# Cross attention and an emulated MXFP8 feed-forward on one Trainium2 core: probabilities scaled in place and turned by float32 transposes with the identity, row-statistics squares kept in the down results' buffer, and every engine's order rewritten

## The chip, the core and the metric

The kernel runs on 1 core of one Trainium2 chip, as five programs side by side: TensorE (PE), VectorE (DVE), ScalarE (ACT), GpSimd (POOL) and SyncE (SP, which here only issues DMAs). The metric is the device time of one execution in microseconds; smaller is better. Before the change it is 609.74 us, the median of 3 runs (608.04 to 609.96).

## What is computed

```
x = x + xattn(layernorm(x), ctx, Wq, bq, Wk, bk)      # x: 4 x 512 x 512, ctx: 4 x 512 x 256
x = x + ffn(layernorm(x), gate_w, up_w, down_w)       # inner size 2048

xattn: query = ctx @ Wq.T + bq;  key = ctx @ Wk.T + bk;  energy = query @ key.T
       attention = softmax(energy, axis=-1);  result = logits @ attention.T
ffn:   gate = mx(x) @ mx(gate_w).T;  up = mx(x) @ mx(up_w).T
       out = mx(silu(gate) * up) @ mx(down_w).T
mx(t): blocks of 32 along the last axis, scale = max|block| / 448, round(t / scale) to float8_e4m3, times scale
```

## The kernel before

Everything is float32 outside and float16 pairs (a high and a low part) inside the feed-forward. There are four batches b of four row tiles of 128 rows, so 16 row tiles r = 4b + lt. The work has these pieces:

- **Attention of batch b** (float32 on PE). `project(b, i)` makes queries and keys of 128 x 512, `energies(b, nt)` a tile of energies, DVE's `row_max` the maximum, ACT's `exponential(b, nt)` the unnormalized probabilities in `probs[b]` with their sum, DVE's `row_sum(b)` the reciprocals. ACT's `weigh(b, nt)` builds a diagonal matrix of 128 x 128 from the identity `idf` and these reciprocals, and PE's `turn_probs(b, nt)` multiplies four blocks of 128 x 128 of the probabilities with it, which turns and normalizes them at once. ACT's `take_probs` copies the result into `AT`, and PE's `attend(b, lt)` (4 matmuls of 128 x 512, at L711) multiplies the input's columns with it. DVE's `add_attended` adds that to the rows, scaled by the reciprocal standard deviation of the row.
- **That deviation** comes from ACT: `row_means(b, half)` and `row_variances(b, half)` pass over the rows with an accumulator; the passes' outputs themselves are never read. The second half ends with a logarithm and an exponential (L975, L976), which give `xrstd_ready`.
- **Quantizing**. Twelve weight units u = 0 to 11 (gate and up of column block c are units 2c and 2c+1, down is 8 to 11), four row batches, and 16 hidden rows go the same way: DVE reduces, scales (L1590, L1537 or L1647), ACT takes magnitudes (L926), DVE rounds (L1458, L1459) and multiplies back (L1605, L1550, L1659). Then the high part is cast by ACT (`unit_hi` L944, `rows_hi` L1074, `hidden_hi` L1114), POOL issues an accumulating DMA that leaves the rest (`unit_rest` L585, `rows_rest` L589, `hidden_rest` L593), the low part is cast (`unit_lo` L950, `rows_lo` L1080), and SP turns both by DMA transposes (L401, L406 for units; L420, L425 for rows; L439, L444 for hidden rows).
- **Feed-forward on PE**. `product(r, c)` is 24 float16 matmuls of 128 x 512 (gate, then up; for each the high rows with high weights, high rows with low weights, low rows with high weights). It waits for `nT_in` (rows turned) and `wT_in` (units turned). `down(r)` is 48 matmuls from the turned hidden row, and `down_last` the same in two halves.

PE's eight banks are given out by a written table `bank_uses`: each string is the list of uses of one bank in order (p, e, t, a for the attention's steps, g and u for gate and up, d for down), and `take_bank` waits until the use ahead of it has been read. The order on each engine is likewise written out call by call; nothing is decided at run time, and an instruction that waits holds all behind it on its engine. SP's and POOL's lists hold the DMAs in the order in which they are issued, with waits between them.

Of the kernel before, what the change touches and what calls it, by code (L numbers as in the profile page):

```python
# [10 lines left out]
ACT = mybir.ActivationFunctionType  # L11
# [21 lines left out]
def xattn_ffn(nc, xrows, xcols, ctxT, consts, units, out):  # L33
# [22 lines left out]
    products = [(3, 0), (1, 0), (0, 0), (2, 0), (3, 1), (2, 1), (6, 0), (6, 1), (4, 0), (4, 1), (5, 0), (2, 2),  # L56
# [5 lines left out]
    nth = {rc: n for n, rc in enumerate(products)}  # L62

    rounds = ("u0 u1 u2 n0 u3 n1 u4 u5 u6 u7 u8 u9 u10 u11 h0 h1 n2 h2 h3 h4 n3 h5 h6 h7 h8 h9 h10 h11 h12 h13 h14"
              " h15").split()
# [3 lines left out]
        ("p0.0 p2.0 e2.0 a0.3 a1.0 a2.2 g1.0 a3.2 g2.1 g4.1 u6.2 g0.2 u0.3 u3.3 u7.1 g8.0 u9.1 g11.0 u12.0 u14.2"  # L69
         " u13.1 g8.2 u10.2 u15.0 d9").split(),  # L70
        ("p0.1 e1.0 e2.1 t1.0 a1.1 t3.0 g0.0 u2.0 g4.0 u2.2 g0.1 u6.3 u1.3 g7.1 d0 g9.1 u10.0 d4 g10.3 u15.1 d11").split(),
        ("e0.0 e1.1 t0.3 a0.2 e3.0 t2.2 a2.0 g3.0 u1.0 g6.0 u4.1 u3.2 u0.2 u1.1 g4.3 u7.2 u8.0 g9.3 g11.1 g12.1"
         " g14.2 u13.0 g12.3 u10.1 d6 g15.3 d14").split(),
        ("e0.1 e1.2 a0.0 t1.3 a1.3 t3.3 a3.3 u2.1 g5.0 g5.1 g5.3 g1.2 u4.2 g7.3 g8.1 g9.2 u11.0 u12.1 g14.3 g13.1"
         " u12.3 g10.2 g15.0 u15.2 d13").split(),
        ("e0.2 e1.3 a0.1 t2.0 t2.3 a2.1 u3.0 g2.0 g6.1 u5.0 g5.2 u5.3 g1.3 u4.3 u7.3 g9.0 u9.3 u11.2 u14.1 g13.0"
         " u13.3 g10.1 u11.3 g15.2 d12").split(),
        ("e0.3 t0.0 t0.2 e2.2 t1.1 t2.1 e3.3 t3.1 u0.0 u6.0 g2.2 u5.1 g6.3 u1.2 g7.0 g2.3 u8.1 g10.0 g11.2 u14.0"
         " u12.2 g13.3 u8.3 g11.3 d8 d15").split(),
        ("p1.0 p2.1 t0.1 p3.1 t1.2 a1.2 t3.2 a3.0 g3.1 u6.1 g6.2 u5.2 g0.3 g3.3 u7.0 u2.3 u9.0 d2 d3 g12.0 g14.1"  # L80
         " g12.2 u13.2 g8.3 d5 g15.1 u15.3").split(),
        ("p1.1 p3.0 e2.3 e3.1 e3.2 a2.3 a3.1 u3.1 u4.0 g3.2 u0.1 g1.1 g4.2 g7.2 d1 u9.2 u11.1 g14.0 u14.3 g13.2"
         " u8.2 u10.3 d7 d10").split(),
# [9 lines left out]
    with ExitStack() as stack:  # L93
# [62 lines left out]
        diagonal = [[h[:, nt, 512 + n * P:512 + (n + 1) * P] for nt in range(LT)] for n in range(B)]  # L156
# [68 lines left out]
        diagonal_ready = sem("diagonal_ready")  # L225
# [105 lines left out]
        def _(sp):  # L331
# [113 lines left out]

            load_slice(0)
            load_ctx(0)
            load_consts()
            load_half(0)
            load_rest(0)  # L450
            load_rows(0)
            load_ctx(1)
            load_unit(1)
            load_ctx(3)
            load_ctx(2)
            load_rows(1)
# [461 lines left out]
        def _(act):  # L918
# [1050 lines left out]
```

## Time and profile before

| | value |
|---|---|
| median of 3 runs | 609.74 us (608.04 to 609.96) |
| profiled execution: span | 608.0 us (the fastest of the three runs took 608.04 us) |
| PE busy | 600.6 us, 99% |
| DVE busy | 484.0 us, 80% |
| ACT busy | 309.2 us, 51% |
| POOL busy | 44.8 us, 7% |
| granted TensorE clock | 0.999 |

The profile gives each engine's busy time, the same in 40 slices of about 15.2 us, the waits with what ended them, and every instruction with its start. A page's matmul durations include the pipeline's depth; the distance from one matmul's start to the next, read from the timeline, is what one costs when they follow each other. Waits that DVE or ACT have cost nothing by themselves while PE goes on.

### The profile page before, as it was taken

How to read it: one execution, taken by the hardware profiler on the slowest of the kernel's cores; microseconds unless marked ns; L12 is line 12 of the kernel's file. 1: busy time of each engine (PE TensorE's matmuls, PEld its weight loads, DVE VectorE, ACT ScalarE, POOL GpSimd, SP SyncE). 2: the span in 40 equal slices, each digit the busy share in tenths (PEclk: the TensorE clock that was granted, in tenths of full speed). 3: DMA queues.
4: the chain of work that ended last, by engine and by line, in shares of the span. 5: the costliest groups of instructions: out<-in, count | busy, mean ns of one | idle time of the engine just before them, and what ended most of it. 6: DMA issues, size and time to landing. Idle time of an engine off the chain costs nothing.

```text
span 608.0 us, 7215 instructions
## 1 busy us (share of the span) xinstructions
PE 600.6 (99%) x2683; PEld 282.3 (46%) x2683; DVE 484.0 (80%) x455; ACT 309.2 (51%) x463; POOL 44.8 (7%) x60
## 2 busy tenths in 40 slices
PE   8999999999999999999999999999999999999998
PEld 3456554444444444444444444444444444444446
DVE  4999998899999999988999985131148899989740
ACT  3999989553555555853475532431121515254520
POOL 0000002100000001010110201000000000001100
PEclk9999999999999999999999999999999999999999
DMA  8989869989988978867445655750010334557691
GB/s 314 396 206 275 234 177 256 280 193 249 208 207 209 219 159 210 174 140 171 124 112 97 148 112 113 165 86 0 1 19 0 53 69 83 90 105 101 110 171 35
DMA packets 148162, 92.28 MB, mean 152 GB/s; under 512 B 134304, under 2 KB 134688, under 8 KB 143264
## 3 DMA queue, kind: packets, MB, share of 16 engines
q1 hardware_dynamic: 142656, 63.78, 45.2%
q0 software_dynamic: 5472, 28.05, 19.9%
q8 instruction: 21, 0.34, 0.2%
q14 instruction: 13, 0.11, 0.1%
HBM read 25.76 MB, written 8.39 MB: 56 GB/s over the span
## 4 chain that ended last, share of the span: by engine, by line
PE 85%; DMA 5%; issue 3%; ACT 3%; DVE 1%; SPq 1%; POOL 0%; DVEq 0%; ACTq 0%
PE bank L727 49%; PE bank L739 17%; PE bank L742 9%; PE bank L711 5%; DMA h<-in_ctxT 2%; PE bank L702 1%; PE bank L695 1%; DMA xT<-hT 1%; PE bank L687 1%; PE bank L757 1%; DMA W<-hT 1%; DMA h<-hT 1%; ACT hT L944 1%; PE bank L762 1%; ACT h L987 0%
## 5 line engine op out<-in xcount | busy, mean ns | idle before, releaser
L727 PE MATMUL bank<-gu_hi,xT 128*128 128x512 f16 x1024 | 243.6, 380 | 1.7 <-DMA xT<-hT 1.7
L727 PEld LDWEIGHTS bank<-gu_hi,xT 128*128 128x128 f16 x1024 | 99.9, 98 | 123.4 <-DMA xT<-hT 3.2
L727 PE MATMUL bank<-gu_lo,xT 128*128 128x512 f16 x512 | 131.5, 379 | 0.0
L739 PE MATMUL bank<-dn,hT 128*128 128x512 f16 x480 | 106.1, 379 | 0.0
L1633 DVE SCALAR_TENSOR_TENSOR h<-bank,unscale,silu 128x512 f32<-128x512 f32 x64 | 47.4, 747 | 56.1 <-PE bank L727 36.1
L1088 ACT ACTIVATE silu<-bank,unscale 128x512 f32<-128x512 f32 x64 | 42.8, 679 | 83.4 <-PE bank L727 40.3
L727 PEld LDWEIGHTS bank<-gu_lo,xT 128*128 128x128 f16 x512 | 50.1, 98 | 60.4
L739 PEld LDWEIGHTS bank<-dn,hT 128*128 128x128 f16 x480 | 47.0, 98 | 56.6
L1114 ACT ACTIVATE W<-h 128x2048 f16<-128x2048 f32 x16 | 30.5, 1909 | 68.3 <-DVE W L1665 25.4
L711 PE MATMUL bank<-dn,h 128*128 128x512 f32 x128 | 55.9, 593 | 0.0
L742 PE MATMUL bank<-dn,hT 128*128 128x512 f16 x240 | 54.3, 379 | 0.0
L1458 DVE SCALAR_TENSOR_TENSOR h<-mag,h 128x2048 f32<-128x2048 bf16 x18 | 41.2, 2288 | 9.4 <-ACT mag L926 9.4
L926 ACT ACTIVATE mag<-h 128x2048 bf16<-128x2048 f32 x18 | 34.2, 1903 | 19.5 <-DVE h L1647 14.1
L1459 DVE SCALAR_TENSOR_TENSOR h<-mag,h 128x2048 f32<-128x2048 bf16 x18 | 41.2, 2292 | 0.6
L926 ACT ACTIVATE mag<-W 128x2048 bf16<-128x2048 f32 x14 | 26.7, 1908 | 23.0 <-DVE W L1590 11.9
L711 PEld LDWEIGHTS bank<-dn,h 128*128 128x128 f32 x128 | 24.3, 190 | 29.8 <-issue 29.4
L1665 DVE SCALAR_TENSOR_TENSOR W<-h,W 128x2048 f16<-128x2048 f32 x9 | 20.6, 2289 | 20.9 <-DMA hT<-W 17.4
L1647 DVE TENSOR_TENSOR h<-h,rscale 128x2048 f32<-128x2048 f32 x16 | 36.7, 2292 | 0.5
L1642 DVE TENSOR_REDUCE hscale<-h 128x64 f32<-128x2048 f32 x16 | 36.5, 2281 | 0.3
L1659 DVE TENSOR_TENSOR h<-h,hscale 128x2048 f32<-128x2048 f32 x16 | 36.6, 2288 | 0.2
L742 PEld LDWEIGHTS bank<-dn,hT 128*128 128x128 f16 x240 | 23.5, 98 | 28.3
L1458 DVE SCALAR_TENSOR_TENSOR W<-mag,W 128x2048 f32<-128x2048 bf16 x14 | 32.0, 2286 | 1.0 <-ACT mag L926 1.0
(119 smaller groups left out, 560.1 us busy)
## 6 DMA issues: line engine op xcount, KB each, us to landing
W<-hT POOLq DMA_DIRECT2D x12, 1024.0 KB, 5.9
W<-in_units SPq DMA_DIRECT2D x11, 1024.0 KB, 5.7
h<-W POOLq DMA_DIRECT2D x7, 1024.0 KB, 6.1
h<-in_xcols SPq DMA_DIRECT2D x4, 1024.0 KB, 12.6
out_y<-y POOLq DMA_DIRECT2D x12, 256.0 KB, 6.2
h<-in_xrows SPq DMA_DIRECT2D x2, 1024.0 KB, 11.8
out_y<-h SPq DMA_DIRECT2D x2, 1024.0 KB, 5.5
h<-hT POOLq DMA_DIRECT2D x2, 1024.0 KB, 5.9
```

Of the source, the lines that this page charges most:

```text
L711: last = pe.matmul(bank[:, :], xTf[b % 2][:, j, lt * P:(lt + 1) * P], AT[:, j, :], start=(j == 0), stop=(j == HT - 1))
L727: last = pe.matmul(bank[:, :], xT[:, b % 2, part, k, :], w[:, c, g, j * 512:(j + 1) * 512], start=(j == 0 and not low), stop=(j == HT - 1 ...
L739: pe.matmul(bank[:, :], hT[:, r % 2, 0, k, :], dn[:, w, k, :], start=(k == 0 and w == 0), stop=False)
L742: last = pe.matmul(bank[:, :], hT[:, r % 2, 1, k, :], dn[:, 0, k, :], start=False, stop=(k == IT - 1))
L926: nc.scalar.activation(mag[:, :], v, ACT.Abs, scale=MAGIC).then_inc(mag_ready, 1)
L1088: nc.scalar.activation(silu[:, n % 2, :], bank_of(f"g{r}.{c}")[:, :], ACT.Silu, scale=unscale[:, 2 * c:2 * c + 1]).then_inc(silu_ready, 1)
L1458: then(dve.scalar_tensor_tensor(v, mag[:, :], floor, v, ALU.max, ALU.add))
L1459: dve.scalar_tensor_tensor(v, mag[:, :], floor, v, ALU.max, ALU.subtract).then_inc(mag_used, 1)
L1633: dve.scalar_tensor_tensor(hrow(r)[:, c * 512:(c + 1) * 512], bank_of(f"u{r}.{c}")[:, :], unscale[:, 2 * c + 1:2 * c + 2], silu[:, n % 2, ...
L1642: then(dve.tensor_reduce(s, blocks(row), AX.X, ALU.max, apply_absolute_value=True))
L1647: dve.tensor_tensor(blocks(row), blocks(row), each_block(rscale[:, :]), ALU.mult).then_inc(hv_ready, 1)
L1659: dve.tensor_tensor(blocks(row), blocks(row), each_block(hscale[:, r % 2, :]), ALU.mult).then_inc(hd_ready, 1)
```

## The change

`turn_probs` transposes blocks of probabilities with the identity instead of multiplying with a diagonal matrix. For that `weigh` now scales the probabilities themselves in place (128 x 512 instead of 128 x 128). `row_means` and `row_variances` leave their unread outputs in `y`, the buffer of the down results with two places, instead of in four places in `h`; with the diagonals also gone from `h`, `hidden_of` (DVE, writes a piece of a hidden row into `h`) needs two waits less. The order of the calls on all five engines, the table of banks and some of the waits between DMAs are new.

```
-        diagonal = [[h[:, nt, 512 + n * P:512 + (n + 1) * P] for nt in range(LT)] for n in range(B)]
...
-                pe.wait_ge(diagonal_ready, LT * b + nt + 1)
+                pe.wait_ge(normal_ready, LT * b + nt + 1)
                 for j in range(HT):
-                    last = pe.matmul(bank[:, j * P:(j + 1) * P], probs[b][:, nt, j * P:(j + 1) * P],
-                                     diagonal[b][nt], start=(j == 0), stop=(j == HT - 1))
+                    last = pe.transpose(bank[:, j * P:(j + 1) * P], probs[b][:, nt, j * P:(j + 1) * P], idf)
...
-                    if lt in copied:
-                        act.wait_ge(act_step, copied[lt])
-                    last = nc.scalar.activation(h[:, lt, 0:512], X[b][:, lt * H:(lt + 1) * H], ACT.Copy,
+                    if lt % 2 in copied:
+                        act.wait_ge(act_step, copied[lt % 2])
+                    last = nc.scalar.activation(y[:, lt % 2, :], X[b][:, lt * H:(lt + 1) * H], ACT.Copy,
...
-                nc.scalar.activation(diagonal[b][nt], idf, ACT.Copy, scale=rsum[:, LT * b + nt:LT * b + nt + 1]
-                                     ).then_inc(diagonal_ready, 1)
+                act.wait_ge(exp_ready, LT * b + nt + 1)
+                nc.scalar.activation(probs[b][:, nt, :], probs[b][:, nt, :], ACT.Copy,
+                                     scale=rsum[:, LT * b + nt:LT * b + nt + 1]).then_inc(normal_ready, 1)
...
-                if r < LT and c == 0:
-                    dve.wait_ge(xrstd_ready, B)
-                elif r < LT and c == 1:
-                    dve.wait_ge(probs_turned, LT * B)
-                elif r < LT and c >= 2:
+                if r < LT and c >= 2:
...
             turn_rows_hi(0)
             turn_rows_lo(0)
-            store_rows(1)
+            turn_unit_hi(2)
+            load_columns(3)
...
             load_unit(6)
+            sp.wait_ge(*rows_rest_in(1))
+            turn_rows_hi(1)
+            turn_rows_lo(1)
             store_rows(3)
             sp.wait_ge(*unit_rest_in(4))
-            turn_rows_hi(1)
-            turn_rows_lo(1)
             turn_unit_hi(4)
             turn_unit_lo(4)
             load_unit(7)
...
             rows_rest(1)
+            unit_max(5)
+            pool.wait_ge(nT_in[1], 32)
             unit_rest(4)
-            unit_max(5)
-            unit_max(6)
```

The order of products changes throughout; its first rows, before and after:

```
-    products = [(3, 0), (1, 0), (0, 0), (2, 0), (3, 1), (2, 1), (6, 0), (6, 1), (4, 0), (4, 1), (5, 0), (2, 2),
+    products = [(3, 0), (1, 0), (0, 0), (2, 0), (3, 1), (0, 1), (6, 0), (2, 1), (5, 0), (6, 1), (4, 0), (5, 1),
+                (1, 2), (1, 1), (0, 2), (4, 2), (5, 2), (2, 3), (0, 3), (6, 2), (1, 3), (2, 2), (5, 3), (6, 3),
```

**PE around the first product.** Before the change PE's list around the first product reads as follows; L702 is `turn_probs` of batch 3 (4 blocks each, 16 in all), L711 `attend` (batch 2 ahead of the products, batch 3 behind), L727 the products (3, 0), (1, 0) and (0, 0).

```order
L711 MATMUL bank<-dn,h 128x512 x16
L702 MATMUL bank<-h,gu_lo 128x128 x16
L727 MATMUL bank<-gu_hi,xT 128x512 x4
L727 MATMUL bank<-gu_lo,xT 128x512 x4
L727 MATMUL bank<-gu_hi,xT 128x512 x8
...
L727 MATMUL bank<-gu_hi,xT 128x512 x4
L711 MATMUL bank<-dn,h 128x512 x16
```

With the change the same place reads (L703 is `turn_probs`):

```order
L711 MATMUL bank<-dn,h 128x512 x16
L703 MATMUL bank<-gu_lo 128x128 x8
L727 MATMUL bank<-gu_hi,xT 128x512 x4
L727 MATMUL bank<-gu_lo,xT 128x512 x4
L727 MATMUL bank<-gu_hi,xT 128x512 x8
...
L703 MATMUL bank<-gu_lo 128x128 x4
...
L703 MATMUL bank<-gu_lo 128x128 x4
...
L711 MATMUL bank<-dn,h 128x512 x16
```

Two of the four turnings of batch 3 have moved behind the first product: one stands behind product (1, 0), the other behind (0, 0), and product (2, 0) now stands ahead of `attend` of batch 3.

**ACT behind the high rows of batch 1.** Before, the three calls behind `rows_hi(1)` (L1074) read as follows (L1088 is the silu of a product, L944 `unit_hi(4)`, L1080 `rows_lo(1)`); `row_variances(3, 1)` with its L975 and L976 stood ahead of the first silu.

```order
L1074 ACTIVATE hT<-h 128x2048
L1088 ACTIVATE silu<-bank,unscale 128x512
L944 ACTIVATE hT<-W 128x2048
L1080 ACTIVATE hT<-h 128x2048
```

With the change (L1075 is `rows_hi(1)`, L987 to L976 are `row_variances(3, 1)`, L1081 is `rows_lo(1)`):

```order
L1075 ACTIVATE hT<-h 128x2048
L1089 ACTIVATE silu<-bank,unscale 128x512
L987 ACTIVATE y,gu_lo<-gu_hi,gu_lo 128x512 x2
L975 ACT_TABLE_LOAD
L975 ACTIVATE gu_lo<-gu_lo,eps 128x4
L976 ACT_TABLE_LOAD
L976 ACTIVATE gu_lo<-gu_lo 128x4
L1081 ACTIVATE hT<-h 128x2048
L944 ACTIVATE hT<-W 128x2048
L1089 ACT_TABLE_LOAD
L1089 ACTIVATE silu<-bank,unscale 128x512
```

The last half of batch 3's row statistics has moved behind the first silus, and with it come three table loads more.

**POOL behind the rest of the rows of batch 1.** Before (L589 is `rows_rest(1)`, the first L585 `unit_rest(4)`, the second `unit_rest(5)`, L575 `unit_max`; in brackets the semaphores that are waited for):

```order
L589 DMA h<-hT 128x2048 [waits nhi_ready,wT_in1]
L585 DMA W<-hT 128x2048 [waits whi_ready]
L575 ISA
L575 ISA umax<-smax 128x1 [waits smax_ready] x2
L585 DMA W<-hT 128x2048 [waits whi_ready,wT_in1]
```

With the change:

```order
L589 DMA h<-hT 128x2048 [waits nhi_ready,wT_in1]
L575 ISA
L575 ISA umax<-smax 128x1 [waits smax_ready]
L585 DMA W<-hT 128x2048 [waits whi_ready,nT_in1]
L585 DMA W<-hT 128x2048 [waits whi_ready,wT_in1]
```

`unit_rest(4)` now waits for the low rows of batch 1 to have been turned (`nT_in1`).

## Rows read from the trace of the kernel before

**Rows 1.** The page: busy time of engines, and granted clock in 40 slices.
```profile
PE 600.6 (99%) x2683; PEld 282.3 (46%) x2683; DVE 484.0 (80%) x455; ACT 309.2 (51%) x463; POOL 44.8 (7%) x60
PEclk9999999999999999999999999999999999999999
```

**Rows 2.** Busy time by stretch (us, engine and count, clock, DMA share, GB/s).
```profile
8.00:93.00 85.00, 82.51 (x287) 44.13 (x286) 81.52 (x103) 77.65 (x176) 5.35 (x9) 1.00 0.90 270
140.00:290.00 150.00, 150.00 (x697) 67.95 (x695) 143.17 (x132) 82.57 (x88) 11.98 (x16) 1.00 0.84 196
290.00:608.00 318.00, 315.07 (x1508) 147.16 (x1505) 216.16 (x178) 117.13 (x163) 19.50 (x22) 1.00 0.45 84
```

**Rows 3.** Timeline of PE: start, duration, instruction, idle before.
```profile
5.87 4.02 PE L687 MATMUL bank<-gu_hi,gu_lo 128*128 128x512 f32 x8
49.83 3.74 PE L702 MATMUL bank<-h,dn 128*128 128x128 f32 x32
53.40 1.06 PE L702 MATMUL bank<-h,gu_lo 128*128 128x128 f32 x8
74.20 13.90 PE L711 MATMUL bank<-dn,h 128*128 128x512 f32 x32
87.94 3.73 PE L702 MATMUL bank<-h,gu_lo 128*128 128x128 f32 x32
92.60 1.04 PE L727 MATMUL bank<-gu_hi,xT 128*128 128x512 f16 x4 [0.93 <-DMA xT<-hT]
138.57 1.04 PE L727 MATMUL bank<-gu_hi,xT 128*128 128x512 f16 x4 [0.32 <-DMA xT<-hT]
603.16 1.91 PE L762 MATMUL bank<-dn,hT 128*128 128x256 f16 x16
```

**Rows 4.** Groups by line and shape: weight loads on PE.
```profile
L727 PEld LDWEIGHTS bank<-gu_hi,xT 128*128 128x128 f16 x1024 | 99.9, 98 | 123.4 <-DMA xT<-hT 3.2 <-issue 0.6
L702 PEld LDWEIGHTS bank<-h,gu_lo 128*128 128x128 f32 x64 | 7.8, 192 | 1.4 <-issue 1.0 <-DVE dn L1504 0.2 <-ACT gu_lo L997 0.2
```

**Rows 5.** Timeline of DVE.
```profile
8.22 1.22 DVE L1569 TENSOR_REDUCE scale<-W 128x32 f32<-128x1024 f32 x1 [7.09 <-DMA W<-in_units]
70.89 2.29 DVE L1550 TENSOR_TENSOR h<-h,xscale 128x2048 f32<-128x2048 f32 x1
112.78 2.29 DVE L1550 TENSOR_TENSOR h<-h,xscale 128x2048 f32<-128x2048 f32 x1
149.97 2.28 DVE L1564 TENSOR_REDUCE scale<-W 128x64 f32<-128x2048 f32 x1
```

**Rows 6.** Timeline of ACT.
```profile
75.44 1.89 ACT L1074 ACTIVATE hT<-h 128x2048 f16<-128x2048 f32 x1
83.56 1.26 ACT L1003 ACTIVATE h<-gu_lo 128x128 f32<-128x128 f32 x4
88.22 1.91 ACT L1080 ACTIVATE hT<-h 128x2048 f16<-128x2048 f32 x1 [1.60 <-DMA h<-hT]
92.34 2.54 ACT L1059 ACTIVATE h<-h,nmean 128x512 f32<-128x512 f32 x4
96.70 1.28 ACT L1088 ACT_TABLE_LOAD   x1
115.11 1.91 ACT L1074 ACTIVATE hT<-h 128x2048 f16<-128x2048 f32 x1 [1.67 <-DVE h L1550]
```

**Rows 7.** Timeline of POOL and of SP's queue: DMA issues.
```profile
82.44 0.88 POOL L589 DMA_DIRECT2D h<-hT  x1 [10.01 <-issue]
124.79 0.86 POOL L585 DMA_DIRECT2D W<-hT  x1 [6.17 <-ACT hT L944]
88.21 1.68 SPq L420 DMA_TRANSPOSE xT<-hT  x1
130.63 4.91 SPq L420 DMA_TRANSPOSE xT<-hT  x1
143.40 0.69 SPq L335 DMA_DIRECT2D W<-in_units  x1
184.97 2.24 SPq L406 DMA_TRANSPOSE gu_lo<-hT  x1
```

More of the change, by code:

```diff
@@ L807, in _ @@
             attend(0, 3)
+            energies(3, 0)
+            energies(3, 1)
+            energies(3, 2)
             turn_probs(1, 0)
@@ L854, in _ @@
+            product(1, 2)
+            product(1, 1)
+            product(0, 2)
+            product(4, 2)
+            product(5, 2)
+            product(2, 3)
+            product(0, 3)
+            product(6, 2)
+            product(1, 3)
+            product(2, 2)
             product(5, 3)
             product(6, 3)
-            product(0, 3)
-            product(1, 1)
-            product(1, 2)
-            product(1, 3)
+            product(3, 2)
+            product(4, 1)
             product(3, 3)
-            product(4, 2)
@@ L877, in _ @@
-            down(2)
-            product(11, 0)
-            product(11, 1)
-            product(11, 2)
-            down(3)
-            down(4)
+            product(10, 1)
+            down(2)
+            product(8, 2)
+            product(10, 0)
+            down(3)
+            product(10, 2)
+            product(11, 3)
+            product(11, 1)
+            product(11, 0)
+            product(9, 3)
+            down(4)
+            down(5)
+            product(13, 0)
+            product(12, 1)
@@ L883, in _ @@
+            product(9, 2)
+            product(11, 2)
+            down(6)
+            product(12, 2)
+            product(10, 3)
+            product(13, 2)
+            product(13, 1)
+            product(13, 3)
             product(12, 0)
-            product(12, 1)
             product(14, 0)
+            product(12, 3)
+            down(7)
             product(14, 1)
+            product(14, 3)
             product(14, 2)
-            product(14, 3)
-            product(12, 2)
-            product(13, 0)
@@ L911, in _ @@
+            down(8)
+            down(9)
+            down(10)
+            product(15, 2)
+            product(15, 3)
+            product(15, 0)
             down(11)
@@ L1365, in _ @@
-            hidden_rescale(6)
+            rows_magnitude(3)
+            silu_of(9, 1)
+            hidden_lo(3)
+            silu_of(10, 1)
+            hidden_unscale(4)
+            silu_of(8, 2)
+            hidden_hi(4)
+            hidden_magnitude(5)
+            silu_of(10, 0)
+            rows_hi(3)
+            silu_of(10, 2)
+            silu_of(11, 3)
+            hidden_rescale(6)
+            hidden_hi(5)
+            hidden_magnitude(6)
+            hidden_lo(4)
+            silu_of(11, 1)
@@ L1369, in _ @@
+            silu_of(11, 2)
+            hidden_magnitude(9)
+            hidden_rescale(9)
+            silu_of(12, 2)
+            silu_of(10, 3)
+            take_down(4)
+            silu_of(13, 2)
+            hidden_hi(7)
+            silu_of(13, 1)
+            take_down(5)
+            hidden_magnitude(10)
+            silu_of(13, 3)
             silu_of(12, 0)
-            hidden_lo(5)
-            silu_of(12, 1)
+            hidden_hi(8)
+            hidden_magnitude(11)
+            hidden_hi(9)
@@ new lines, in _ @@
+            hidden_rescale(11)
+            hidden_hi(10)
+            hidden_unscale(8)
+            take_down(8)
+            silu_of(14, 2)
+            silu_of(15, 1)
+            hidden_unscale(9)
+            hidden_rescale(12)
+            hidden_hi(11)
+            hidden_magnitude(13)
+            take_down(9)
+            hidden_rescale(13)
+            hidden_hi(12)
+            hidden_unscale(10)
+            silu_of(15, 2)
+            hidden_unscale(11)
+            hidden_rescale(14)
@@ L1436, in _ @@
+            hidden_unscale(12)
+            hidden_hi(13)
+            take_down(10)
+            silu_of(15, 3)
+            silu_of(15, 0)
+            take_down(11)
+            hidden_unscale(13)
+            hidden_rescale(15)
+            hidden_magnitude(14)
+            hidden_magnitude(15)
+            hidden_hi(14)
+            take_down(12)
+            take_down(13)
+            hidden_unscale(14)
+            hidden_hi(15)
+            add_constant()
+            take_down(14)
             hidden_unscale(15)
-            hidden_hi(15)
```

794 lines of the change are left out of this document (354 added, 440 removed), and 9 rows, old and new, of the table products.

## The prediction, made blind

> **What bounds the kernel now.** I read the page first. PE is busy for 600.6 of 608.0 us and the granted clock is full in every slice, which is the 2.4 GHz level [rows 1]. Then the stretches: from 140 to 290 us PE runs 697 matmuls in 150.00 us, and the rest of the kernel looks the same [rows 2], so from there on PE is the bound and nothing that another engine does is seen. The last matmuls start at 603.16 us [rows 3]; the 3 us behind them are the last sums and the store. The stretch ahead of 93 us is different: DVE is busy for 81.5 and ACT for 77.7 of 85 us beside PE's 82.5 [rows 2]. Three engines are full there at once, and the reader should ask of each of them what it could do if the others were faster.
>
> The first product starts at 92.60 us, after 0.93 us of waiting for turned rows [rows 3]. From there to the end PE waits 0.32 us and hardly more. So the span is (start of the first product) + 515.4 us, of which nearly all is matmuls that the change keeps. This one moment, call it T1, is where the change must be read.
>
> T1's chain: DVE multiplies the rows of batch 0 back, ends at 73.1 [rows 5]; ACT casts them, 75.44 to 77.3 [rows 6]; POOL issues the accumulating DMA at 82.44, it lands at about 88.2, where SP turns the rows [rows 7]; 4.4 us later the product starts.
>
> **The change, part by part.**
>
> *The transposes.* Before, 32 records (16 blocks of 128 x 128) start 3.57 us apart (49.83 to 53.40 [rows 3]): 0.223 us a block, 14.3 us for 64. The trace has no transpose in the transposing mode, so I bound it. Above: the same 0.223 us. Below: a float16 matmul is one pass, 150 us / 697 = 0.215 us for 512 columns, so 128 columns in one pass are 0.054 us. A weight load takes 98 ns in float16 and 192 ns in float32 [rows 4], and one must go with each block. I take 0.1 us, nearer to the low end, since a block then needs one load and one pass. PE's work falls by 64 x 0.12 = 7.9 us, with ends of 0 and 10.8 us.
>
> A rule speaks to this. The Trainium skill, page "TensorE: Matmul & The Clock Gate", section "Terms", calls the transpose mode 4 times faster for FP32. By it a block would be 0.056 us and PE's work 10.7 us less; no row here shows it. If that were all, the span would be 597.3 us.
>
> *But PE's saving lies ahead of T1 and PE doesn't set T1.* Ahead of the first product PE had 83 us of work in 86.7 us. Now it has 73 us (two turnings of batch 3 stand behind it), and T1 waits for DVE and ACT.
>
> *DVE up to the rows of batch 0.* The calls ahead of and with the multiplying back of batch 0 are the same 45 before and now, in another order. They take 64.9 us from 8.22 us on [rows 5], of which some 2 us are waits (1.0 for a magnitude, 0.8 for an attended bank, and small ones). Without any wait they end at 71.1, as before at 73.1. Walking through both lists with the durations of the trace I get one wait of about 1 us for the magnitude of the rows, and 72.5.
>
> *ACT up to casting these rows.* Two calls are moved behind (two halves of variances, 1.4 and 1.9 us, -3.3 us). All 12 `weigh` of batches 0 to 2 stand ahead of it; each grows from 1.26 / 4 = 0.31 us to 2.54 / 4 = 0.63 us, the price of four 128 x 512 passes [rows 6]: +3.8 us. Net +0.5 us on an engine that was busy 62 of 67 us. The walk gives a start of the cast at 73.4 against 75.44, with ends of 71 (no waits at all) and 76. The squares that go to `y` cost nothing: same instructions, and ACT executes them one after the other anyway. So the cast ends at 75.2, 2.1 us earlier.
>
> *The DMA.* Before, 5.1 us passed between the end of the cast and POOL's issue, though POOL shows nothing else [rows 6, 7], then 5.8 us of flight. For batch 1 the issue follows the cast at once. Before, SP had issued a slow load of columns (12.6 us is the median of that kind) just ahead; now that load stands behind the turning of the rows. I take 7 us from the cast to landing instead of 10.9: 82.2 (as before: 86.1). Now PE's list has two turnings of batch 3 ahead of product (3, 0), and their `weigh` stand on ACT behind the low rows, which wait for this landing: 1.8 + 1.5 (means) + 0.4 + 2 x 0.6 us, then the turnings, 0.4. T1 = 82.2 + 5.3, with the hand-overs between engines (some 0.1 us each) and the SP's transpose in parallel (4.4 us) about 88.5. With 86.1 it would be 92. `attend` of batch 2 (13.7 us [rows 3]) ends at 85.6 and doesn't hold it. **T1: -4.1 us**, with ends -6 and 0.
>
> *What is late next.* Two things are due: rows of batch 1, needed by product (6, 0), and the weight units. Up to product (6, 0) PE has attend of batch 3 (13.7) and six products (5.18 each): T1 + 45.3 = 133.8. SP turned these rows at 130.63, behind a store and the rest of unit 4 [rows 7]; now right after their own rest. DVE's list ahead of them has two pieces of hidden rows and one unit's reduction more (+2.9 us), against 4.1 us of waits that it had between 73 and 115. I keep DVE's end at 115.0 as before [rows 5]; cast 1.9, DMA 7, and the turning lands at 129, its low part at 134, which is needed at 135.5. No wait.
>
> Three table loads of 1.28 us [rows 6] come in by the late `row_variances(3, 1)`: they lie on ACT between 117 and 126, where ACT was half idle. They hold `xrstd` of batch 3 until 122; DVE's first addition of batch 3 waits some 1 us, and PE's banks don't need it sooner.
>
> Units 6 and 7 are the tight place. Product (2, 3) is now 18th behind T1, where before a product with c = 3 came 19th: it is due at T1 + 0.4 + 13.7 + 17 x 5.18 = T1 + 102.2 = 190.7; before at 200. Unit 7's low part was turned from 184.97 on [rows 7] and lands 4.3 us later, at 189.3. POOL's new wait puts the rest of unit 4 behind the turned low rows of batch 1: 134 instead of 124.79 [rows 7]. Its buffer then takes unit 7, whose load was issued at 143.40 and which DVE reduces from 149.97 on [rows 5]. Now: rest landed 141, low part 143, turned from 144, load issued 146 and landed 152. DVE gets 2 us later there, and unit 7 lands at about 192. **Wait of PE: +1.1 us**, with ends 0 and 5.
>
> *Two turnings behind T1*: 8 x 0.05 to 0.1, **+0.4 us**. The end is unchanged: four `down` and the last one lie behind the last product, 41 us, and by the rows' durations the last hidden row is turned some 39 us behind it. The rewritten bank table holds 64 x 2 uses of the same lengths; where it is tight (product (0, 0) takes the bank of (3, 0)'s up at T1 + 10.4 = 98.9, which DVE leaves at about 98.8), a us late on DVE is a us lost on PE.
>
> **Sum.** 608.0 - 4.1 + 1.1 + 0.4 = 605.4 us against the profiled execution; that was the fastest of three runs and 1.7 us below their median. Against the median: 609.7 - 2.6 = 607.1, and if the waits behind T1 come out shorter than I let them, 606. I predict 606.5.
>
> **Rivals.**
> 1. *PE's saving arrives in full* (the skill's factor of four, and DVE and ACT follow). For it: all lists are new, so the others may have been rearranged to follow. Against it: the same 45 calls on DVE ahead of T1. T1 can't come before 71.1 + 1.9 + 6.5 + 5.3 = 84.8, so the most is 7.8 us: 602. Chance 0.08.
> 2. *The transposes cost what the matmuls did.* Then PE has 81 us ahead of T1, plus about 1.5 us of waiting for the second context, which it now needs before its first energies. T1 would be 90 to 91, the time 608.5. Chance 0.08.
> 3. *ACT is the bound ahead of T1.* It is full in my walk, and each wait it has there goes to T1; if the DMA takes 10.9 us again, T1 is 92 and the gain is gone: 609.5. For it: the 5.1 us are unexplained. Chance 0.16.
> 4. *Slower: unit 4's rest.* If turning the low rows of batch 1 lands at 138 instead of 134 (it was issued at 135.65 before), units 4, 5 and 7 all come 4 us later, and PE, now due at 190.7 instead of 200, waits 5 us or more at product (2, 3), and about 2 at (1, 2), due at T1 + 76: 608.0 - 4.1 + 0.4 + 7, and 1.7 to the median: 613. It decides from the point where that landing is more than 5 us late. Chance 0.12.
> 5. The forecast, a T1 3 to 5 us earlier with 0 to 2 us given back: 0.56, with a range of 604.5 to 608.
>
> **Numbers.** Within 0.3% (1.8 us: 607.9 to 611.6) a measurement can't tell from no change. Faster: 0.52 of the forecast's 0.56, rival 1, and a part of rivals 2 and 3: 0.64. Slower: 0.12. Same: 0.24. The range reaches from rival 1's middle to rival 3: 603 to 610.
>
> **What would show it.** Right: the first L727 matmul at 87 to 90 us; PE's busy time ahead of it about 10 us shorter than the stretch, in several gaps of 1 to 3 us; L703 blocks under 0.12 us apart; four table loads; the clock still full. The DMA of the rows of batch 0 issued less than 1 us behind its cast. Wrong: T1 at 92 or later (rival 3), L703 at 0.22 us (rival 2), or a wait of PE for `wT` near 165 or 190 us of more than 3 us (rival 4).

## The result, and the profile after

The changed kernel takes 615.92 us (median of 4 runs, 612.96 to 620.36) against 609.39 us (4 runs, 608.04 to 609.96): a ratio of 1.0108, with an interval of 1.0077 to 1.0139. It is 1% slower. The forecast was 606.5 us, with a range that ended at 610.

The profiled run of the changed kernel is the slowest of the four: 620.36 us, with a span of 618.6. All its runs are 1.75 us longer than their spans, and those of the kernel before 1.8 to 2.2 us longer. So the span of 608.0 us of the kernel before belongs to a run of 609.7 to 610.0 us, near its median, and not to the fastest run. First the page: busy times and clock [against rows 1], and the shares of the chain that ended last.

```profile
PE 600.1 (97%) x2619; PEld 274.9 (44%) x2619; DVE 483.8 (78%) x455; ACT 316.5 (51%) x466; POOL 48.7 (8%) x60
PEclk8999999999998999999999999999999998999999
PE 49%; DVE 15%; ACT 12%; DMA 11%; issue 10%; SPq 3%; POOL 1%; DVEq 0%; ACTq 0%; POOLq 0%
```

PE does 64 matmuls less and is as long busy as before. Its clock, full before, is not full in three slices. Its timeline has the reason (start, duration, instruction, count, idle before it):

```profile
11.98 3.60 PE L688 MATMUL bank<-gu_hi,gu_lo 128*128 128x512 f32 x4 [2.92 <-DMA gu_hi<-in_ctxT]
15.41 3.60 PE L696 MATMUL bank<-gu_lo 128*128 128x512 f32 x8
...
88.96 1.25 PE L703 MATMUL bank<-gu_lo 128*128 128x128 f32 x8
90.05 1.03 PE L727 MATMUL bank<-gu_hi,xT 128*128 128x512 f16 x4
...
126.48 1.02 PE L727 MATMUL bank<-gu_hi,xT 128*128 128x512 f16 x4 [0.94 <-DVE gu_hi L1505]
...
191.95 1.07 PE L727 MATMUL bank<-gu_hi,xT 128*128 128x512 f16 x4 [2.78 <-DVE h L1630]
192.81 1.91 PE L727 MATMUL bank<-gu_lo,xT 128*128 128x512 f16 x4
194.52 2.73 PE L727 MATMUL bank<-gu_hi,xT 128*128 128x512 f16 x8
...
305.82 1.04 PE L727 MATMUL bank<-gu_hi,xT 128*128 128x512 f16 x4 [0.55 <-ACT silu L1089]
...
398.12 1.24 PE L739 MATMUL bank<-dn,hT 128*128 128x512 f16 x5 [1.48 <-DMA hT<-W]
...
512.61 1.04 PE L727 MATMUL bank<-gu_hi,xT 128*128 128x512 f16 x4 [2.97 <-ACT silu L1089]
```

The first product starts at 90.05 us, 2.55 us earlier than before [rows 3]. Up to there the change gains time, as forecast. Behind it the kernel needs 618.6 - 90.05 = 528.5 us, where it needed 515.4: 13.1 us more. Adding up how far starts of matmuls lie apart beyond the usual (0.216 us, and 0.43 for float32 ones of 128 x 512), PE loses 13.1 us there, where before it lost 1.1; the two turnings behind the first product are another 0.9 (8 blocks of 0.109). 12.0 and 0.9 account for all but 0.2 us.

3.2 of the 13.1 us are no waits. The matmuls at 192.81 start (194.52 - 192.81) / 4 = 0.43 us apart, twice the usual. The stretches of 10 us show the lower level of the clock (the last three columns are granted clock, DMA share and GB/s); the share of 0.83 is a mixture of both levels:

```profile
0.00:10.00 10.00, 7.88 (x19) 2.93 (x19) 1.07 (x2) 2.66 (x3) 0.35 (x7) 1.00 0.80 251
10.00:20.00 10.00, 8.02 (x15) 3.60 (x16) 7.84 (x11) 4.39 (x9) 0.38 (x1) 0.83 1.02 414
190.00:200.00 10.00, 8.05 (x30) 3.40 (x31) 8.88 (x7) 5.76 (x6) 0.87 (x1) 0.83 1.04 263
510.00:520.00 10.00, 7.39 (x27) 3.06 (x28) 5.00 (x6) 5.28 (x6) 0.00 (x0) 0.83 0.00 0
```

Each of the three follows a wait of PE of 2.8 to 3.0 us. The four runs order themselves by this: granted clock 0.992 in the run of 620.36 us, 0.994 in 616.76, 0.997 in 615.08, and 1.000 in 612.96. The run at full clock is 3.6 us slower than the kernel before, the median 6.5: so about half of the median's loss is there without any lower clock. The rest is in the main the clock: the three stretches at the lower level cost the profiled run 1.6 + 3.2 = 4.8 us of the 7.4 between it and the fastest; what the other 2.6 are isn't shown.

**The wait at 189 us, read back.** POOL's queue, ACT and DVE (apart, in order of time):

```profile
176.89 1.90 ACT L944 ACTIVATE hT<-W 128x2048 f16<-128x2048 f32 x1
179.43 0.87 POOL L585 DMA_DIRECT2D W<-hT  x1 [13.73 <-ACT hT L944]
188.35 1.91 ACT L950 ACTIVATE hT<-W 128x2048 f16<-128x2048 f32 x1 [3.32 <-DMA W<-hT]
190.17 0.67 ACT L1089 ACTIVATE silu<-bank,unscale 128x512 f32<-128x512 f32 x1
191.05 0.75 DVE L1630 SCALAR_TENSOR_TENSOR h<-bank,unscale,silu 128x512 f32<-128x512 f32 x1 [2.61 <-ACT silu L1089]
```

The high part of unit 7 is cast, its rest travels for 8.9 us (the one before it, issued at 163.83 us, took 5.8; why isn't shown), and ACT stands before `unit_lo(7)`. Behind that call stands `silu_of(0, 2)`, whose product PE has long finished; behind the silu DVE's `hidden_of(0, 2)`, which frees the bank that product (5, 2) needs. PE doesn't wait for unit 7 itself, which product (2, 3) needs one product later; it waits for a bank, through two lists.

**The wait at 509 us** has the same form:

```profile
502.22 2.29 DVE L1662 SCALAR_TENSOR_TENSOR W<-h,W 128x2048 f16<-128x2048 f32 x1 [9.18 <-DMA hT<-W]
504.43 2.28 DVE L1639 TENSOR_REDUCE hscale<-h 128x64 f32<-128x2048 f32 x1
507.69 2.29 DVE L1644 TENSOR_TENSOR h<-h,rscale 128x2048 f32<-128x2048 f32 x1
510.07 1.91 ACT L926 ACTIVATE mag<-h 128x2048 bf16<-128x2048 f32 x1 [17.01 <-DVE h L1644]
511.89 1.25 ACT L1089 ACTIVATE silu<-bank,unscale 128x512 f32<-128x512 f32 x2
```

DVE waits 9.2 us in `hidden_lo(9)` until a turned hidden row leaves its place; `hidden_scale(12)` stands behind; ACT waits 17 us for it with the magnitude of row 12, and the silus of (14, 1) and (14, 3) stand behind the magnitude. The smaller gap at 126 us is of this form too: ACT's `row_variances(3, 1)`, now among the silus, loads tables at 120.88 and 122.49 us, so that DVE's additions of batch 3 come late and hold their banks.

The table of banks can make such chains bite. Before, it dealt the uses evenly, 21 to 27 a bank; now banks 0, 1 and 3 have 33 to 37 uses, bank 6 has 8. Around 189 us only banks 0, 1, 3 and 7 take turns.

### The profile page after: what moved, and what is told of

Read it like the earlier page. It is cut to its first block, busy times and chain, and to the rows that moved or that the text cites. A ratio compares the mean times of both kernels' runs of the same rounds, so it can differ in the third digit from the quotient of the medians.

```text
span 618.6 us, 7100 instructions
## 1 busy us (share of the span) xinstructions
PE 600.1 (97%) x2619; PEld 274.9 (44%) x2619; DVE 483.8 (78%) x455; ACT 316.5 (51%) x466; POOL 48.7 (8%) x60
## 4 chain that ended last, share of the span: by engine, by line
PE 49%; DVE 15%; ACT 12%; DMA 11%; issue 10%; SPq 3%; POOL 1%; DVEq 0%; ACTq 0%; POOLq 0%
PE bank L727 25%; PE bank L739 12%; PE bank L742 6%; DMA hT<-W 4%; ACT mag L926 3%; PE bank L711 2%; DVE h L1630 2%; DVE W L1459 1%; DMA W<-hT 1%; DMA gu_hi<-in_ctxT 1%; DMA h<-W 1%; ACT y L987 1%; DMA W<-W 1%; SPq L424 1%; PE bank L757 1%
## 5 line engine op out<-in xcount | busy, mean ns | idle before, releaser
L727 PE MATMUL bank<-gu_hi,xT 128*128 128x512 f16 x1024 | 246.4, 381 | 7.4 <-ACT silu L1089 3.7
L727 PEld LDWEIGHTS bank<-gu_hi,xT 128*128 128x128 f16 x1024 | 100.0, 98 | 131.1 <-issue 9.8
L727 PE MATMUL bank<-gu_lo,xT 128*128 128x512 f16 x512 | 133.0, 383 | 0.0
L727 PEld LDWEIGHTS bank<-gu_lo,xT 128*128 128x128 f16 x512 | 50.4, 98 | 60.9 <-issue 1.0
L711 PE MATMUL bank<-dn,h 128*128 128x512 f32 x128 | 56.1, 594 | 1.3 <-ACT dn L1011 1.3
L1132 ACT ACTIVATE y<-bank,xnmr,odown 128x128 f32<-128x128 f32 x48 | 18.0, 456 | 40.6 <-PE bank L742 40.6
L711 PEld LDWEIGHTS bank<-dn,h 128*128 128x128 f32 x128 | 24.1, 190 | 31.7 <-issue 28.5
```

What stands on the lines that cost most here:

```text
L711: last = pe.matmul(bank[:, :], xTf[b % 2][:, j, lt * P:(lt + 1) * P], AT[:, j, :], start=(j == 0), stop=(j == HT - 1))
L727: last = pe.matmul(bank[:, :], xT[:, b % 2, part, k, :], w[:, c, g, j * 512:(j + 1) * 512], start=(j == 0 and not low), stop=(j == HT - 1 ...
```

## Experiments

Each ran beside the kernel before, whose medians were 609.4 to 609.7 us. Ratios are to the kernel before. Line numbers shift by a few where the table of banks or the content differs.

**e1_content: the content alone.** Before's orders, table and waits, with the changed `turn_probs`, `weigh`, `row_means`, `row_variances` and `hidden_of`.

```
-    last = pe.matmul(bank[...], probs[b][:, nt, ...], diagonal[b][nt], start=(j == 0), stop=(j == HT - 1))
+    last = pe.transpose(bank[...], probs[b][:, nt, ...], idf)
...
-    nc.scalar.activation(h[:, lt, 0:512], ...)
+    nc.scalar.activation(y[:, lt % 2, :], ...)
```

> The kernel before with every order, wait between DMAs and bank use as it was, and only the content of the change: float32 transposes with the identity, the probabilities scaled in place, squares in the down results' buffer, two waits less in hidden_of. Theory A (the orders and the bank table lose the time, the content is innocent): PE saves up to 7.3 us ahead of the first product but waits there for ACT and DVE; weigh adds 0.32 us each on a full ACT, so the first product moves by -1 to +2 us and the time is 608 to 611. Theory B (the content itself costs): as late as the changed kernel or later, 613 or more. Theory C (the saving of the transposes was there to be had in the old orders): 602 to 606.

Measured: 610.70 us, ratio 1.0019 (1.0005 to 1.0032). PE around the first product, in this kernel:

```profile
90.72 1.91 PE L701 MATMUL bank<-gu_lo 128*128 128x128 f32 x16
92.47 1.02 PE L725 MATMUL bank<-gu_hi,xT 128*128 128x512 f16 x4
...
95.36 1.90 PE L725 MATMUL bank<-gu_hi,xT 128*128 128x512 f16 x8 [1.01 <-DMA xT<-hT]
```

PE has 7 us of work less, and the first product starts where it did [rows 3]; then PE waits 1 us for the low rows. Two things in this profile need sorting out. First, the clock was at its lower level shortly ahead, and from there to the first product PE has no gap:

```profile
73.46 3.65 PE L694 MATMUL bank<-gu_lo 128*128 128x512 f32 x4
70.00:80.00 10.00, 8.38 (x22) 3.64 (x21) 9.92 (x15) 9.87 (x25) 0.85 (x1) 0.83 0.96 255
```

At full clock PE would have been ready 1.7 us sooner, at 90.8 us. But the high rows landed at 91.03 and the low rows at 95.32 us (before: 92.56 and 94.94), so PE would have waited for the low rows that much longer, as far as these landings don't themselves hang on PE. Second, the runs of this kernel at a granted clock of 1.000 took 609.5 to 610.2 us, no less than the kernel before. So Theory A holds: the content costs next to nothing and brings nothing in these orders. The loss is in the orders and the table.

**e2_matmul: the changed kernel without the transposing mode.**

```
-    last = pe.transpose(bank[...], probs[b][:, nt, ...], idf)
+    last = pe.matmul(bank[...], probs[b][:, nt, ...], idf, start=(j == 0), stop=(j == HT - 1))
```

> The changed kernel with turn_probs as ordinary float32 matmuls with the identity (0.22 us a block as in rows 3, against 0.109 us). If PE's work ahead of the first product is on its path in the new orders, up to 0.113 x 56 = 6.3 us come back: a first product at 92 to 96 against 90.05, and 618 to 622. If ACT and DVE set it, the first product stays within 1 us of 90 and the time is that of the changed kernel, 615 to 616.

Measured: 621.95 us (618.84 to 626.61), ratio 1.0202 (1.0163 to 1.0241). The first product starts at 93.59 us against 90.05, so here PE's work was on the path; 3.5 of the 6.3 us arrive. Of the other 2.5 us, 0.9 are the two turnings behind the first product (8 blocks of 0.113 more). The rest is in stalls that have shifted: in its profile the gap near 512 us is 5.3 us with twice as long a stretch of lower clock behind it, one of 1.4 us is new at 257 us, and those at 126 and 398 are gone.

**e4_silu: ACT's order at 189 us.**

```
-            unit_lo(7)
             silu_of(0, 2)
+            unit_lo(7)
```

> The changed kernel with ACT's silu of product (0,2) ahead of the cast of unit 7's low part instead of behind it. Theory A (an in-order list and a nearly used-up set of banks): PE's gap at 189 to 192 us (2.95 us and some 1.7 us of lower clock behind it) goes, unit 7 is still turned at about 194.6, ahead of product (2,3)'s need at about 196; the time falls by 3 to 5 us, to 611 to 613. Rival (unit 7 itself is late, so the wait only moves to product (2,3)): a gap of 2 us or more named wT near 195, and 614 or more.

Measured: 615.08 us (613.30 to 617.69), ratio 1.0087 (1.0063 to 1.0112). Neither theory's number. The gap at 189 us went, and no lower clock came there. But the next silus stand behind `unit_hi(8)`. PE and ACT in its profile:

```profile
195.22 1.02 PE L727 MATMUL bank<-gu_hi,xT 128*128 128x512 f16 x4 [0.64 <-ACT silu L1089]
...
189.33 1.90 ACT L926 ACTIVATE mag<-W 128x2048 bf16<-128x2048 f32 x1
192.01 1.91 ACT L944 ACTIVATE hT<-W 128x2048 f16<-128x2048 f32 x1 [0.78 <-issue]
193.83 1.25 ACT L1089 ACTIVATE silu<-bank,unscale 128x512 f32<-128x512 f32 x2
```

Three gaps of 0.8, 0.6 and 0.5 us take the place of one of 2.95. Behind the first product its profile needs 525.2 us, 3.3 less than the changed kernel's, although the lower clock behind its gap at 505 us lasts twice as long; but the medians are only 0.8 us apart, less than the runs of either scatter, so the size of the gain is not settled.

**e5_banks: the table dealt out anew**, behind `attend` of batch 3: each use takes the bank that has been free longest. One bank before and after:

```
-        ("t0.2 p3.1 e2.2 e3.0 t2.1 e3.3 u3.0 g0.0").split(),
+        "t0.2 p3.1 e2.2 e3.0 t2.1 e3.3 u3.0 g0.0 g0.1 g6.1 g1.1 g2.3 g2.2 g4.1 g7.1 g8.3 g8.1 u8.2 g11.1 d5 d7 d8 u15.0".split(),
```

> The changed kernel with the same orders, and the table of banks behind attend of batch 3 dealt out anew, so that each use takes the bank longest free (22 to 29 uses a bank; in the changed kernel 8 to 37). Theory A (the uneven table leaves PE one product of slack, so a silu or an addition 3 us late is 3 us of PE's): the gaps at 126, 189, 305 and 509 us go, with the lower clock behind two of them; only the wait for a turned hidden row near 397 (1.5 us) stays; 13 us of gaps and lower clock behind the first product fall to about 3, and the time to 605 to 608. Rival (banks don't matter, the late silu would stop PE anyway): gaps stay where they are and the time is 614 to 617.

Measured: 614.38 us (612.14 to 616.34), ratio 1.0067 (1.0042 to 1.0093). The gaps at 126, 189, 305 and 397 us went, as Theory A had it (those at 126, 305 and 397 are missing from the profile of e6, below, too, which has the old table; so of these only the one at 189 us can be put down to the table). The one at 509 stayed, with the lower clock behind it, and a new one came at 343 us (1.6 us, mended in e10):

```profile
506.42 1.68 PE L720 MATMUL bank<-gu_hi,xT 128*128 128x512 f16 x4 [2.98 <-ACT silu L1082]
```

There the silu of (14, 1) comes 18 us behind its product (gate ready at 487.7, silu at 505.7), and no table covers that. Theory A had put too much on the table: the time fell by 1.5 us where it expected 8 to 11, and with the intervals of both ratios overlapping even that is not clear of noise.

**e6_scale: DVE's order at 502 us.**

```
-            hidden_lo(9)
             hidden_scale(12)
+            hidden_lo(9)
```

> The changed kernel with DVE's hidden_scale(12) ahead of hidden_lo(9), which in the changed kernel waits 9.2 us for a turned hidden row with the scale, the magnitude and the silu of product (14, 1) queued behind it. Theory A: the gap at 509.5 to 512.6 us (3.1) and the 1.5 us of lower clock behind it go, the others stay: 610.5 to 612.5. Rival (the whole chain of hidden rows is late there, and another link stops PE): a gap of 2 us or more between 495 and 530 and 614 to 616.

Measured: 610.80 us (608.39 to 614.60), ratio 1.0028 (1.0009 to 1.0047): Theory A. One call moved by one place on DVE, and the median is 5.1 us lower; by the intervals of the two ratios that is 3 to 7 us. The changed kernel's profile has 3.1 us of gap and 1.5 of lower clock there, which is what the call can give back. Its runs at a granted clock of 1.000 took 608.4 to 610.9 us, against 612.96 of the changed kernel's one such run. The gaps at 126, 305 and 397 us, which lie ahead of the moved call, are missing from its profile as well, and one of 0.8 us is new at 242: such small gaps come and go between executions. Its profile had the first product earlier, too, though nothing ahead of it was changed:

```profile
11.75 1.96 PE L688 MATMUL bank<-gu_hi,gu_lo 128*128 128x512 f32 x4 [2.72 <-DMA gu_hi<-in_ctxT]
13.54 3.60 PE L696 MATMUL bank<-gu_lo 128*128 128x512 f32 x8
...
88.15 1.03 PE L727 MATMUL bank<-gu_hi,xT 128*128 128x512 f16 x4
...
91.36 1.90 PE L727 MATMUL bank<-gu_hi,xT 128*128 128x512 f16 x8 [1.32 <-DMA xT<-hT]
...
190.33 1.02 PE L727 MATMUL bank<-gu_hi,xT 128*128 128x512 f16 x4 [3.04 <-DVE h L1630]
```
```profile
10.00:20.00 10.00, 8.25 (x20) 3.72 (x20) 9.44 (x12) 6.26 (x15) 0.38 (x1) 1.00 1.02 413
190.00:200.00 10.00, 9.67 (x45) 4.31 (x46) 9.93 (x9) 4.08 (x4) 0.86 (x1) 1.00 1.04 270
```

The wait for the second context at 9 us is the same as in the changed kernel, but the clock stayed full behind it: four float32 matmuls take 13.54 - 11.75 = 1.79 us instead of 3.43. These 1.6 us (and 0.2 of an earlier landing) pass through 75 us of work of three engines undiminished in this pair of profiles: 88.15 against 90.05. The wait at 187 us also left the clock full here.

**e3_start: the start as before.**

```
-            load_consts()
-            load_ctx(0)
             load_slice(0)
+            load_ctx(0)
+            load_consts()
...
-            project(1, 0)
             energies(0, 0)            # ... to energies(0, 3)
+            project(1, 0)
```

> The changed kernel with its start as before: the slice of the first weights loaded ahead of the constants and the first context, and project(1, 0) behind the four energies of batch 0 (with its use of a bank moved to fit). Theory S (what the start loses is carried down ACT's and DVE's full lists to the first product): DVE's first reduction at 8.2 instead of 9.2 us, the wait of 2.9 us for the second context gone, the first product 1 to 1.5 us earlier than 90.05, the time 614 to 615. Rival (the full engines take the start's loss up, or the low rows' turning holds the first product anyway): the first product at 89.5 to 90.5 and 615 to 616.

Measured: 616.53 us (614.24 to 620.46), ratio 1.0118 (1.0088 to 1.0147), first product at 89.64. A trial with a fault of its own: I had given project(1, 0) a bank that is free only after an exponential, so PE's wait moved instead of going:

```profile
16.91 3.27 PE L688 MATMUL bank<-gu_hi,gu_lo 128*128 128x512 f32 x7 [2.86 <-ACT dn L997]
```

**e7_three and e8_all: mends together.** e7_three has the edits of e4, e5 (with other banks from down(2) on) and e6; e8_all has the start of e3 as well.

> Three mends at once on the changed kernel: the table of banks dealt out anew (as in the run of that alone, but the bank of down(2) and those behind it chosen otherwise), silu of (0, 2) ahead of unit 7's low part, hidden_scale(12) ahead of hidden_lo(9). The run with the banks alone still had behind the first product 1.2 us (rows turned late, at 91), 1.6 us (down(2) for a bank, at 343) and 3.2 and 1.5 us (silu at 503, then lower clock). Theory A: only the 1.2 us at 91 stay; 614.4 less 6.2: 607 to 609. Rival (each mended wait gives way to another of its size): 611 to 614.

> The three mends and the start as before. If the start is carried down to the first product, 1 us less than the three mends, 606 to 608, and the first product at 88 to 89; else the same as with three. Below 608 the new orders would keep something of what the transposes save; at 609.5 nothing.

Measured: 609.24 us (608.00 to 610.67), ratio 0.9997 (0.9984 to 1.0009), and 611.75 us, ratio 1.0034 (1.0022 to 1.0046). Three mends together bring the new orders back to where the kernel before was; how much each gives among the others wasn't run. e8_all carries the fault of e3: its first product is at 91.75 us, 4 us later than in e7_three (87.72), with the wait of 3 us and a lower clock (0.93 up to 20 us) at the start.

**e9_start2: the start, now with a free bank** (bank 6) for project(1, 0), and its taking behind `unit_magnitude(0)`, on top of e7_three.

> The three mends and the start as before, this time with a bank for project(1, 0) that is free from the outset and its taking ahead of the exponentials; the two earlier trials of the start gave it a bank that was free only after an exponential, and PE waited 3 us there. Theory S (a PE wait for the second context at 9 to 12 us, with the lower clock that sometimes follows it, is carried down to the first product): no PE wait over 1.5 us ahead of 20 us, the first product at 86 to 87.5, and 607.5 to 608.5 against 609.24 of the three mends. Rival (ACT and DVE are full and the turning of the low rows holds the product): the first product waits for xT longer instead, 609 to 609.5.

Measured: 607.75 us (607.20 to 608.95), ratio 0.9968 (0.9956 to 0.9980). The time is Theory S's, 1.5 us less than e7_three's. But its first product, at 87.60 us, is not earlier than in e7_three's profile, which had kept a full clock: what the mend gives is that the early wait of 3 us is gone, and with it the chance of a lower clock behind it. All nine of its runs have a granted clock of 1.000, while eight of e7_three's twelve have 0.997.

**e10_down: take_down(2) behind silu_of(9, 1) on ACT**, on top of e9.

```
-            take_down(2)
             hidden_rescale(5)         # ... rows_magnitude(3), silu_of(9, 1)
+            take_down(2)
```

> The same, with ACT's take_down(2) behind the silu of (9, 1) instead of ahead. In the kernel with three mends DVE waited 9.8 us for the magnitude of rows 3, which stood on ACT behind take_down(2), and PE waited 1.6 us near 342 for a bank that DVE left late. Theory: that gap goes and the time is 1.6 us less than the same kernel without it (606 to 607). Rival: another link is as late, less than 0.5 us.

Measured: 606.19 us (606.08 to 606.37), ratio 0.9941 (0.9926 to 0.9956), 1.6 us less than e9. This version beats both kernels. It still has the new order of products and the new waits between DMAs, POOL's wait for `nT_in` among them, so these didn't need to be undone. Its page, and PE behind the first product:

```profile
PE 594.9 (98%) x2619; PEld 274.0 (45%) x2619; DVE 483.8 (80%) x455; ACT 316.9 (52%) x466; POOL 50.2 (8%) x60
PEclk9999999999999999999999999999999999999999
```
```profile
88.12 1.03 PE L720 MATMUL bank<-gu_hi,xT 128*128 128x512 f16 x4
...
91.11 1.90 PE L720 MATMUL bank<-gu_hi,xT 128*128 128x512 f16 x8 [1.11 <-DMA xT<-hT]
```

Here the mode's saving is visible at last: PE is busy for 5.7 us less than before [rows 1], and its six runs lie within 0.3 us of each other.

**e11_turn: the turning of unit 2's high part ahead of the rows' of batch 0** on SP, on top of e10.

> The same, with the turning of unit 2's high part issued ahead of the turning of rows of batch 0 (as in the kernel before) instead of right behind it. The low rows' turning took 6.8 us there against 4.2 at most before. If it is slowed by its neighbour, PE's wait for xT behind the first product (1.4 us) goes, 1 to 1.4 us less; if the unit's turning now delays the rows' own, the first product comes later, and the time rises by 1 to 2 us; if neither, no difference.

Measured: 607.99 us (606.92 to 608.66), ratio 0.9972 (0.9962 to 0.9983), 1.8 us worse than e10. PE's wait for the low rows went, but the rest of the rows came 1.1 us later and with it the first product (89.22), and PE waited 1.3 us near 193 us for unit 7. The second of the three forecasts held, and the trace shows the way: the rest of unit 2, issued at 68.85 us beside the moved turning, took 8.5 us instead of 6.2 and landed at 77.37, and POOL issued the rows' rest only at 77.62, though ACT had cast their high part by 75.44.

The low rows' turning took 4.9 us here and 6.6 in e10. That the turning right behind it slows it is not shown: of the profiles with that same order on SP, e5 to e10 have 6.5 to 6.8 us, but the changed kernel, e2, e3, e4 and e12 have 4.7 to 4.9.

**e12_mends_matmul: e10 with ordinary matmuls in turn_probs.**

> The kernel with all mends (not the one about the turnings), but turn_probs as ordinary float32 matmuls with the identity, as in the earlier run of that on the changed kernel, where it cost 6 us with its stalls. Here the lists behind the first product have slack, so only the first product counts: 56 x 0.113 = 6.3 us of PE's work come back ahead of it, of which PE's idle time there takes up some; 2 to 4 us slower than the kernel with all mends, 608.5 to 610.5. If PE's work ahead of the first product is free, less than 0.5 us slower.

Measured: 609.50 us (608.64 to 610.39), ratio 0.9992 (0.9981 to 1.0003): 3.3 us above e10, with no run of the one inside the range of the other. Its first product starts 3 us later:

```profile
91.10 1.03 PE L721 MATMUL bank<-gu_hi,xT 128*128 128x512 f16 x4
```

## Why the prediction was wrong

*The transposes: right.* I took 0.1 us a block; the timeline of the changed kernel has 8 blocks in 90.05 - 88.96 = 1.09 us, 0.136 each with a hand-over, and 12 in a row at 26.85 us take 1.31 us, 0.109 each. The Trainium skill's factor of 4 (page "TensorE: Matmul & The Clock Gate", section "Terms") is a factor of 2 here.

*The first product: 1.5 us off, by what happens at the start.* The forecast was 88.5 us, the profile has 90.05. DVE's first reduction is at 9.21 us instead of 8.22 [rows 5], PE waits 2.9 us at 9 to 12 us for the second context, and a lower clock follows. I had priced neither the loads, though their new order stands in the diff, nor the clock; the wait for the context I had named only in rival 2, with 1.5 us. ACT, DVE and POOL's queue around the rows of batch 0:

```profile
73.56 2.29 DVE L1551 TENSOR_TENSOR h<-h,xscale 128x2048 f32<-128x2048 f32 x1
...
76.20 1.89 ACT L1075 ACTIVATE hT<-h 128x2048 f16<-128x2048 f32 x1
...
78.48 0.88 POOL L589 DMA_DIRECT2D h<-hT  x1 [6.12 <-ACT hT L1075]
```

DVE ends at 75.8 (forecast 72.5) and the cast at 78.1 (75.2). The DMA's part was right, and better than let: POOL issues 0.4 us behind the cast instead of 5.1, and SP turns the rows at 84.29, 6.2 us behind the cast (forecast 7, before 10.9).

Those 5.1 us, which the prediction left unexplained, have a partner in the trace of the kernel before: the rest of unit 2, the DMA that POOL had issued just ahead. Issued at 71.57 us, it took 10.6 us and landed at 82.18; POOL's issue came at 82.44. SP had issued a load of columns at 70.83 us, which was under way beside it until 78.97; with the change that load stands behind the turning of the rows, and unit 2's rest took 6.0 us. That the load is what slowed it wasn't tested. (First the kernel before, then the changed one.)

```profile
71.57 0.85 POOL L585 DMA_DIRECT2D W<-hT  x1 [23.09 <-DMA gu_hi<-hT]
DMA to landing us min/median/max: 10.6/10.6/10.6
DMA to landing us min/median/max: 6.0/6.0/6.0
```

In every profile of this case, the issue of the rows' rest comes 0.25 to 0.4 us behind the later of two things, the rows' cast and the landing of unit 2's rest; in the kernel before, e1, e2 and e11 it is the landing. The program has no wait between the two DMAs, so why POOL holds the second one isn't shown, and it is no rule for all of POOL's DMAs: at 241.93 us, before the change, one is issued 2.2 us ahead of the landing of the one before it.

With a full clock at the start the same code up to the first product has it at 88.15 (e6) and 87.72 us (e7). Then the low rows: I let their turning pass in parallel in 4.4 us; in e6 it took 6.8 (from 84.55), and PE waited 1.3 us. The kernel before has such a wait too, which I left out when I wrote that PE waits 0.32 us and hardly more behind the first product:

```profile
94.99 1.90 PE L727 MATMUL bank<-gu_hi,xT 128*128 128x512 f16 x8 [0.49 <-DMA xT<-hT]
```

The term T1, -4.1 us, was -2.55.

*"Wait of PE: +1.1 us": here it failed.* The term stood for everything that PE would lose behind the first product; with the 0.4 us of the turnings I had 1.5 us there, and the profile has 13.1 more than before. I looked only for arrivals that PE itself waits for, `nT_in` and `wT_in`. Of those there is none of size: no wait for batch 1's rows, as forecast, and none for a unit, where I had put the 1.1 us. But PE has a third need, a free bank, and that passes through ACT's and DVE's lists. Unit 7's rest was later than I had walked it (its low part was turned from 190.4 us on, where I had it landed at 192; rival 4 had such a lateness, from another cause), and it stopped PE through the silu behind `unit_lo(7)`, at product (5, 2) and not at (2, 3). The walk of the hidden rows in the second half, "the end is unchanged", was made for the last row only: 3 us of wait at 509 us, and 1.5 at 398. Only the wait at 398 was for a turned row; the one at 509 was again for a bank.

*"PE's banks don't need it sooner" (the table loads): wrong.* DVE's first addition of batch 3 was 1 us late, as forecast, and that cost PE 0.9 us in the profiled run. In e6, whose first product came 1.9 us earlier, the same lists had no such gap.

*The table of banks.* I called it rewritten with the same uses and checked one pair. I should have counted: 8 uses in one bank and 37 in another. e5 is the measure of it: 5.4 us less behind the first product in the profile, but 1.5 in the median, which is not clear of noise.

*The clock.* The forecast had "the clock still full" as a condition and no price. Three stretches at the lower level are 4.8 of the 7.4 us between the fastest and the slowest run of one kernel. The gap of 2.95 us at 189 us cost 4.6 with what followed it.

*Rivals.* Rival 1 (the saving in full) is refuted by a first product at 90.05 us against its 84.8, and by e1; rival 2 (no saving in the mode) by the blocks' 0.109 us. Rival 3, ACT and DVE as the bound ahead of the first product, is what e1 shows in the old orders: 7 us of PE's work less, and no gain. In the new orders half of it arrives (e2: 3.5 of 6.3 us; e12: 3.0). Rival 4 had the sign right and the size near (613), and that was luck, since its mechanism isn't the one that acted: unit 4's rest was issued at 132.47 us, before the 134 of the forecast.

So the change is made of orders ahead of the first product that make use of the transposes, worth some 3 us, and of lists and a table that lose 13 us behind it in the profiled run. The mends show that the two can be parted: 615.9 to 606.2 us with the same content.

## What to carry to other kernels

When the order of in-order engines changes, walk every list for calls that wait for a DMA or for a late reduction and ask which short call behind them frees a buffer of the bounding engine; a silu of 0.7 us behind a cast that waits comes as late as the cast. Count how evenly the buffers are dealt, since that is the slack that covers such waits: in e5 it took away the wait at 189 us, though not the one at 509, where a silu came 18 us late. And where an engine saves work, first find what its neighbours wait for: a saving ahead of a shared landing is worth nothing until the order lets the others follow.

## What was not expected of the hardware

- A wait of PE of about 3 us leaves the clock full in one run and at the 1.2 GHz level in the next, with the same code: behind the wait at 9 to 12 us the granted clock is 0.83 in one profile and 1.00 in another, behind that at 188 us likewise. A kernel with such waits scatters: 612.96 to 620.36 us for the changed kernel, 606.08 to 606.37 for e10_down, which has none. That isn't the only source of scatter: the kernel before, with no wait of PE near 3 us, ranged from 608.2 to 611.8 in 26 runs.
- Shorter waits can be followed by the lower level too: in e1 it came at 73.5 us behind waits of 1.17 and 0.44 us, in e4 at 57 us behind one of 1.30 us. In both PE's last work before it was transposes of probabilities; whether that plays a part isn't shown.
- A float32 transpose of 128 x 128 with the identity costs 0.109 us from start to start, half of the 0.223 us that the float32 matmul of the same block costs.
- An accumulating DMA of 1 MB took 5.8 us at 78 us and 8.9 us at 179 us in one profile, and 10.6 us at 72 us in the kernel before; the mean of the kind wouldn't have shown it.
